# Attention: the maximum products placed by the work they give VectorE, not at even distances

## The reference, cut to what matters

```python
x = x + 0.5 * _L0_ffn_ref(_layernorm(x), ...)
x = x + _L0_attn_ref(_layernorm(x), ...)
...
def _L0_attn_ref(x, w_in, b_in, w_out, b_out):
    qkv = x @ w_in.T + b_in
    q, k, v = jnp.split(qkv, 3, axis=-1)
    q, k, v = (to_heads(q), to_heads(k), to_heads(v))
    scores = jnp.einsum('bhqd,bhkd->bhqk', q * scale, k)
    scores = scores + causal_bias
    attn = jax.nn.softmax(scores, axis=-1)
    out = jnp.einsum('bhqk,bhkd->bhqd', attn, v)
    out = out.transpose(0, 2, 1, 3).reshape(bsz, slen, esz) @ w_out.T + b_out
    return jnp.where(jnp.isnan(out), 0, out)
```

## Time and profile before

| | |
|---|---|
| median of 3 runs | 1777.79 us (1774.81 to 1777.92) |
| profiled execution | 1778.24 us, its span on the core 1776.5 us |
| TensorE busy | 1634.1 us (92%) |
| VectorE busy | 1287.4 us (72%) |
| ScalarE busy | 1017.1 us (57%) |
| GpSimd busy | 776.3 us (44%) |
| maximum products on TensorE (L1049) | 768, 250.1 us |
| masked parts on VectorE (L1285) | 512, 234.0 us with the readings |
| plain reductions on VectorE (L1287) | 256, 161.1 us |

### The profile page before, as it was taken

The page is one execution under the profiler, slowest core; times in us unless marked ns, Lnnn a source line. Parts: engine busy times, 40 slices in busy tenths (PEclk is TensorE's granted clock), DMA queues, the critical chain, the costliest instruction groups (busy, mean ns, idle before and its releaser), DMA issues. The chain is left out here.

```text
span 1776.5 us, 25917 instructions
## 1 busy us (share of the span) xinstructions
PE 1634.1 (92%) x8360; PEld 1160.4 (65%) x8360; DVE 1287.4 (72%) x3879; ACT 1017.1 (57%) x1718; POOL 776.3 (44%) x734
## 2 busy tenths in 40 slices
PE   3999879899999989997999999999998988999998
PEld 2777645555556555554777767777777876777776
DVE  4777658788778878872777767777765876767775
ACT  3666415565566566665666646555555645555554
POOL 1566611311311312112566646555574625555555
PEclk9999958999999999998999999999999998999999
DMA  4222211111111112101233332111110002111120
GB/s 149 76 87 88 91 33 24 21 30 24 23 32 22 25 20 35 20 11 42 75 121 120 103 100 83 54 49 48 49 48 1 1 1 90 60 55 60 55 94 20
DMA packets 58246, 95.01 MB, mean 53 GB/s; under 512 B 9312, under 2 KB 17120, under 8 KB 58112
## 3 DMA queue, kind: packets, MB, share of 16 engines
q1 hardware_dynamic: 56000, 91.07, 18.1%
q10 hardware_dynamic: 2112, 2.30, 0.4%
HBM read 76.76 MB, written 2.88 MB: 45 GB/s over the span
## 5 line engine op out<-in xcount | busy, mean ns | idle before, releaser
L695 DVE TENSOR_TENSOR big<-banks,big 128x512 f32<-128x512 f32 x384 | 264.7, 689 | 211.5 <-ACT banks L632 175.5
L1157 ACT ACTIVATE big<-banks 128x1024 f32<-128x1024 f32 (+3 forms) x384 | 301.8, 811 | 172.9 <-PE banks L1068 167.0
L632 ACT ACTIVATE banks<-banks 128x512 f32<-128x512 f32 x384 | 223.9, 583 | 275.9 <-PE banks L575 270.6
L705 DVE TENSOR_TENSOR big<-big,banks 128x512 f32<-128x512 f32 x400 | 274.9, 687 | 29.8 <-PE banks L578 15.8
L1049 PE MATMUL banks<-arena 128*128 128x512 f32 (+3 forms) x768 | 250.1, 402 | 27.1 <-DVE att_mx L1285 15.4
L1197 POOL TENSOR_SCALAR_AFFINE_SELECT big<-big 128x512 f32<-128x512 f32 x128 | 81.6, 637 | 401.9 <-ACT big L1157 401.9
L1285 DVE CUSTOM_DVE_ANT_0 banks<-banks,att_mask 128x128 f32<-128x128 f32 (+3 forms) x512 | 234.0, 525 | 28.9 <-PE banks L1049 28.2
L665 POOL TENSOR_TENSOR ffn1b_hid_l<-big,ffn1b_hid_h 128x512 fp32r<-128x512 f32 x128 | 165.6, 1294 | 128.6 <-ACT ffn1b_hid_h L637 128.6
L1068 PE MATMUL banks<-arena 128*128 128x512 f32 (+3 forms) x768 | 206.3, 354 | 12.1 <-ACT big L1157 12.0
L665 POOL TENSOR_TENSOR ffn1a_hid_l<-big,ffn1a_hid_h 128x512 fp32r<-128x512 f32 x128 | 165.5, 1293 | 118.3 <-ACT ffn1a_hid_h L637 118.3
L575 PE MATMUL banks<-xh,arena 128*128 128x512 f32 x512 | 208.9, 408 | 8.3 <-PEq L1451 6.9
(11 more groups left out here) (256 smaller groups left out, 3175.8 us busy)
## 6 DMA issues: line engine op xcount, KB each, us to landing
big<-weight_rows SPq DMA_DIRECT2D x256, 128.0 KB, 2.9
big<-weight_rows SPq DMA_DIRECT2D x128, 256.0 KB, 4.2
arena<-att_parts SPq DMA_DIRECT2D x16, 384.0 KB
arena<-att_parts SPq DMA_DIRECT2D x128, 48.0 KB
w_raw<-in_ffn_w_dram SPq DMA_DIRECT2D x12, 256.0 KB, 2.9
out_dram<-x SPq DMA_DIRECT2D x8, 256.0 KB, 2.3
setup_raw<-in_ffn_w_dram SPq DMA_DIRECT2D x3, 576.0 KB, 7.2
gau_angle<-in_consts_dram SPq DMA_DIRECT2D x2, 512.0 KB, 7.2
```

The source lines that it names most:

```text
L632: act.activation(gate if c < NSCALED else sil, gate, ACT.Silu).then_inc(silu_done, 1)
L695: dve.tensor_tensor(scl[:, num % 2, :], gate_ps[:, num % NB, :], share[:, c // PER, :], ALU.mult)\
L705: dve.tensor_tensor(hid[:, num % NH, :], scl[:, num % 2, :] if c < NSCALED else sil, up_ps[:, num % NB, :], ALU.mult).then_inc(hidden, 1)
L1157: act.activation(probs[:, unit % NPROB, 2 * pair:2 * pair + 2, 0:c], score_ps[:, pair, :, 0:c], ACT.Exp, scale=SCALE).then_inc(exped, 1)
```

## The change

Two lines are added and one is altered. Each class of `MAXB` gets an effort: its columns, plus for each part 128 where the part has no mask and 256 where it has. `reached` is the effort that lies ahead of each piece, and the piece's time is set in proportion.

```diff
     def order():
 
 
+        effort = [sum(width_of(t, c) + (P if c < t // TG else 2 * P) for t, c in parts) for parts in MAXB]
+        reached = [sum(effort[:i]) * HG + j * effort[i] for i in range(len(MAXB)) for j in range(HG)]
         weight = [columns(u) + P for u in range(NU)]
...
             for i in range(len(MAXB)):
                 for j in range(HG):
-                    put(n - 1.18 + 0.93 * (i * HG + j) / (len(MAXB) * HG), "max", n, j, i)
+                    put(n - 1.18 + 0.93 * reached[i * HG + j] / (sum(effort) * HG), "max", n, j, i)
```

## The result

The changed kernel takes 1791.12 us (median of 5, 1788.0 to 1793.47) where the kernel before, run beside it, takes 1774.81 (1772.14 to 1777.92). The ratio is 1.0082, 95% interval 1.0064 to 1.01: slower by some 14.6 us (the two medians as such are 16.3 apart). Slower was forecast, but +5.9 us, and the time lies above the range. Of all executions timed here one, of E10, took 2584.58 us at a mean granted clock of 0.56, and the ratio leaves it out.

The account below looks back on a forecast made before the run. TensorE sets the pace, with VectorE full in u0 to u3. A plain section's terms, 1.76 - 1.48 + 0.32 = +0.60 us, with the other kinds of section gave +5.9 us: 1783.7 us, range 1777.5 to 1789.

Parts of the forecast that it names:

- What bounds the kernel: TensorE sets the pace; VectorE is full in u0 to u3; about 1.6 us a section can be lost u4 to u9.
- First stretch: From u11 to the `pv` of u3: three more pieces at nearly VectorE's price, +1.76 us a plain section.
- two runs of seven reductions: Sign expected on VectorE in the first stretch, with the `pv` of u1 between them.
- Second stretch: From the `pv` of u3 to the first pair of u9: three pieces leave and waits shrink, -1.48 us.
- wait before class 8: Sign: TensorE's wait of 0.24 us before a piece of class 8 would be gone.
- exponential of u8: Sign: the wait of 0.4 us for ScalarE before the first pair of u9 would still be there.
- Third stretch: Behind `maxt`: fourth piece of class 0 joins the third and delays the pair of u10, +0.32 us.
- No DMA "changes place": No DMA is moved and the one behind the turned maxima (`maxt`) has as long as before, so no DMA cost counted.
- Sections 2, 6 and 10 "as long as before": Sections with projections, VectorE idle in the first stretch: +1.05 and -1.37 in the first two stretches, sum 0.
- Faster: Rival: VectorE has 1.06 us to spare in u11 to u3; -0.46 a plain section, 1772 us; chance 0.10.
- Nothing measurable: Rival: `pv` time takes up half of the pieces, or only plain sections pay; 0 to +3.4 us; chance 0.24.
- A plain piece holds its bank longer than 0.62 us: Rival: reductions in longer runs take 0.65 to 0.66 us, +5 us more, 1789 us; chance 0.08.

Follow-up runs that it names:

- E10: Changed kernel with keys' first two DMAs released earlier and one piece ahead of each `pv` except u9's: 1776.72 us, 1.0001.
- E4: Changed kernel with plain reductions reading half their columns: 1767.38 us, 0.9956.
- E6: Changed kernel with effort spacing for classes 0 to 4 only, classes 5 to 8 at even distances: 1790.5 us, 1.0079.
- E9: Kernel before with keys' first two DMAs released earlier and one piece ahead of each `pv` in u3, u5, u7, u11: 1768.0 us, 0.9955.
- E3: Changed kernel with only the four pieces of class 0 back at even distances: 1786.5 us, 1.0058.
- E2: Kernel before with the keys' first two DMAs released by the first pair of scores, not the second: 1776.2 us, 0.9996.
- E1: Changed kernel with the keys' first two DMAs released by the first pair of scores, not the second: 1783.75 us, 1.0048.
- E8: Kernel before with keys' first two DMAs released earlier and the first piece of class 0 ahead of the `pv` of u9: 1782.13 us, 1.003.
- E11: E9 with the statistics of the next batch moved from u5 to u2, against the kernel before: 1764.0 us, 0.9929.

## Why the prediction was right or wrong

**What bounds the kernel: right.** VectorE is full in u0 to u3 and late in u4 to u8. E4 shows the first half of that, the third columns of E6 and E9 the other.

**First stretch, +1.76: measured +1.63.** The two runs of seven reductions with the `pv` of u1 between them are there, at 0.60 us from start to start ((4.28 - 0.68) / 6) instead of 0.62. The 0.62 divided the 6.18 us of ten reductions by ten; from start to start they too are 0.61 ((6.18 - 0.68) / 9). That is little of the 0.13: the fourteenth piece starts 7.72 after the first where 7.75 was forecast. Most of it lies behind that piece, where the `pv` follows 0.60 later (540.92 to 541.52) and the prediction counted 0.70.

**Second stretch, -1.48: measured -1.59** (541.52 to 557.59, 16.07, against 17.66). The wait before class 8 is gone. The one shown for the exponential of u8 is 0.18 instead of the 0.4 expected, but the pair before it was late too, so that the first pair of u9 still starts 0.92 after the last of u8, where 0.46 would do.

**Third stretch, +0.32: measured +0.55**, and E3 gives 0.54 by itself. The steps were right up to the fourth piece (0.64 behind the third, forecast 0.65). The mistake is in the end of the term: I let only the pair of u10 behind it be late. But that pair's exponential is late with it, and the first pair of u11 waits for the exponential of the pair that had its banks. It starts at 531.19, 0.44 after the piece ahead of it (530.75), where before it was 0.23 (555.80 to 556.03). ScalarE of the changed kernel, and the wait of that pair's weights in 529.8 to 531.6 us:

```profile
530.54 1.57 ACT L1159 ACTIVATE big<-banks 128x512 f32<-128x512 f32 x3 [0.79 <-PE banks L1070]
...
PEld banks L1070 <- ACT big L1159: 0.4, 1, 0.4
```

That is most of the 0.23 a section that was missed, which the first two terms, together 0.24 lower than forecast, take back.

**No DMA "changes place", and "so the DMA behind them has as long as before": this step failed.** It is the one that put the time outside the range: it set the DMAs at nothing. The prediction looked at the DMA behind `maxt` alone. It had a queue whose order does not change, and took that for a queue whose deadlines do not change. The keys' DMA starts at u7 and is needed at the end of the `pv` of u9; the change shortens what lies between by 0.6 us, and it had next to no slack (0.04 by E2). Taken as a chain (0.70 to the first issue, 2.83 of issues, 2.19 from there to the first user: 5.72), it would have given a floor for u7 to class 0, and any gain behind u7 would have been set to 0. That is +0.6 in fourteen sections, 8.7 us. The two waits for this DMA in the trace of before were the sign of it. E1 takes the wait away, and E2 shows that before it was 1.0 us in all.

With the keys out of the way the plain section is as forecast, 32.28 against 32.3. The sum is near, the phase between the first and last `maxt` +5.7 and the run 0.0048 (8.5 us, some 2 either way) against +5.9, but that is luck in part. By kinds of section in E1: plain sections +0.52 to +0.61 (forecast +0.60), section 9 with statistics +0.37 (+0.38), projections -0.04 to -0.05 (0), section 14 +0.66 (+0.28), `wo` +0.23, +0.26 and -0.04 (+0.47). Sections 1 and 5, with statistics, are +0.9 and +1.9 (+0.38): each has a stretch at half clock, which the execution of the kernel before has in none of the sections 1 to 14, and the two bring about 2.8 of the 5.7. Against that, the stretch from the first `maxt` to the second is -0.66 (section 0: +0.7). There too the clock has a part: it rose 7.3 us behind the first `maxt` before, and 6.0 behind it in E1.

The changed kernel's own +16.8 between the first and last `maxt` divides so, by estimate: 8.4 are the waits for the keys (9.4 against 1.0), some 3.8 three stretches at half clock (1.4, 1.4 and 1.1 by the lengths of like sections), and 4.6 are left for the moved pieces, where +5.9 was forecast.

**Sections 2, 6 and 10 "as long as before": not in the change** (42.47 against 41.95 in section 6), since the keys' wait is in them too; in E1 it holds, 41.90.

**The rivals.** Faster: fell with the first stretch. Nothing measurable: fell. "A plain piece holds its bank longer than 0.62 us" gave 1789, the nearest of all the times, and its mechanism is false: the longer runs are no slower, 0.60. The Trainium skill's figure for PSUM (page "Perfetto Trace Analysis", section "Optimizing Scalar/DVE Operations", about 125 ns) would have brought it. By this trace's 1.04 ns a column, 512 columns are 0.53, which leaves 0.07 of the 0.60: here too the trace decides against it. A time that comes out near a rival is no evidence for the rival. The time to explain came by way of a DMA, and no rival had one.

## What to carry to other kernels

Before you count a gain in a stretch, look for transfers that are issued inside it by one step and needed by another behind it. A transfer that shows no wait may be one that lands just in time, and its issue, its length and its landing are then a floor under that stretch; the test is the distance from the releasing instruction to the first user in rows of before, against the same distance in work. And work spread "evenly by cost" is not spread by slack: in E9 a piece was cheap ahead of a long step of TensorE that gives VectorE nothing to do, and in the change it was dear in a stretch where VectorE, which empties its bank, was already without gaps. Last, before two executions are compared to 1 us, look at the granted clock of the same sections in both.

## What the runs showed of the hardware that was not expected

- The four transfers of the keys are issued at 0.71 us each, and where the first user of the last one waits for it, it starts 2.13 to 2.23 us after its issue has ended in thirteen of the changed kernel's fourteen sections (2.20 in the one above, 558.45 to 560.65), and 2.59 in one; in E8's row it is 2.18. A chain of four short DMAs is thus 5.0 us from its first issue to use.
- A wait that the records give as 0.15 or 0.16 before a maximum product costs more than that. In the changed kernel two pieces that both waited so start 0.64 apart (529.07 and 529.71), where two free ones start 0.23 apart, and the second takes 0.34 until the next start (530.05).
- TensorE's granted clock falls to half for short stretches within the phase. Windows of the changed kernel in sections 5 and 13; the row 1 us ahead of the first stretch, a row within the second, and one of section 9:

```profile
473.43:476.84 3.41, 3.41 (x14) 2.32 (x17) 3.33 (x18) 2.05 (x2) 3.31 (x6) 0.50 0.00 0
746.50:749.91 3.41, 3.41 (x17) 2.40 (x21) 2.62 (x6) 1.58 (x3) 1.21 (x2) 0.50 0.04 10
...
472.40 0.55 PE L1051 MATMUL banks<-arena 128*128 128x128 f32 x2 [1.92 <-DVE att_mx L1287]
...
746.80 0.63 PE L1070 MATMUL banks<-arena 128*128 128x256 f32 x2
...
620.55 0.55 PE L1051 MATMUL banks<-arena 128*128 128x128 f32 x2 [1.94 <-DVE att_mx L1287]
```

  The column behind POOL is the clock: 0.50, the lower of its two levels, 1.2 GHz and not 2.4. A pair of 256 columns takes 0.63 there where it takes 0.40 at 530.05. This is why sections of one kind differ within one execution: in the changed kernel section 5 takes 36.25 and section 9, at full clock, 34.88; section 13 takes 34.08 and section 11 32.96; in E1 sections 5 and 9 take 35.82 and 34.29. One stretch costs 1.1 to 1.5 us. Section 1 of the change (37.25) has a stretch and the keys' wait of 1.6.
- What TensorE did before such a fall: in sections 1 and 5 it had stood 1.94 and 1.92 us for VectorE, behind the statistics, and ahead of section 13 0.99 us for the keys. Not each such pause is followed by a fall: section 9 of the change has the same 1.94 and none, and the kernel before stood 2.25 without one. E11, whose longest waits for VectorE before a maximum product are 0.7 and 0.9, has no fall between 276 and 781 us. How often the other executions of each kernel have such stretches is not known, since one of each was profiled; so how much of a ratio is theirs stays open. The columns are from sections at full clock and hold without it.
